# The class row joins the recurrent layer's output in TensorE's accumulation, instead of being added on GpSimd

## The reference

```python
ewma = (forward_ewma(x) + backward_ewma(x)) * 0.5
h = ewma @ W.T + b                               # 256 features
hidden = layernorm(h)
for l in range(2):                               # recurrent layers of 64 states
    delta = softplus(hidden @ Wd[l] + bd[l]); u = hidden @ Wi[l] + bi[l]
    decay = exp(-delta * softplus(A_log[l])); drive = delta * u
    hs, final = scan(decay, drive)               # s = d * s + g over 750 positions
    y = hs @ Wo[l] + bo[l]
    class_state = final @ Ws[l] + bs[l]          # one row of 256 per sequence
    hidden = y + class_state[:, None, :]
h = h + hidden
x2 = layernorm(h)
out = h + shared_mlp(x2) + routed_mlp(x2)        # 16 experts, 4 of them per position
```

## Time and profile before

| what | us |
|---|---|
| three timed runs | 1349.87, 1364.24, 1368.43 |
| median | 1364.24 |
| profiled execution, its own time | 1353.63 |
| its span, first to last instruction | 1351.8 |
| TensorE busy | 1192.3 (88%) |
| VectorE busy | 943.9 (70%) |
| ScalarE busy | 549.4 (41%) |
| GpSimd busy | 479.7 (35%) |

### The profile page before, as it was taken

The page is one execution under the profiler, slowest core; times in us unless marked ns, Lnnn a source line. Parts: engine busy times, 40 slices in busy tenths (PEclk is TensorE's granted clock), DMA queues, the critical chain, the costliest instruction groups (busy, mean ns, idle before and its releaser), DMA issues.

```text
span 1351.8 us, 24750 instructions
## 1 busy us (share of the span) xinstructions
PE 1192.3 (88%) x7477; PEld 1075.1 (80%) x7477; DVE 943.9 (70%) x2326; ACT 549.4 (41%) x899; POOL 479.7 (35%) x329
## 2 busy tenths in 40 slices
PE   4469859978999799977999899977999899999997
PEld 3358648768987689866988789867988789899997
DVE  6886996986479865897578864797658763654443
ACT  1525623622455235432366235452355343223332
POOL 2053382153315432164403623173412712163333
PEclk8659878988999899998999899997899899999999
DMA  3230021022323112231222303231122312244331
GB/s 105 47 86 23 28 83 31 27 74 56 51 41 88 44 22 47 40 93 48 25 63 57 88 10 52 40 93 41 13 48 39 90 37 24 42 125 71 51 52 21
DMA packets 88288, 71.48 MB, mean 53 GB/s; under 512 B 39671, under 2 KB 82848, under 8 KB 88168
## 3 DMA queue, kind: packets, MB, share of 16 engines
q1 hardware_dynamic: 58832, 43.30, 11.9%
q0 software_dynamic: 26832, 26.06, 11.7%
q10 hardware_dynamic: 2504, 0.55, 0.2%
HBM read 31.36 MB, written 39.34 MB: 52 GB/s over the span
## 4 chain that ended last, share of the span: by engine, by line
PE 62%; DVE 14%; issue 10%; POOL 9%; ACT 4%; DMA 0%; POOLq 0%; ACTq 0%; DVEq 0%
PE gu_ps L1669 18%; PE gu_ps L1642 13%; PE d_ps L1729 9%; PE d_ps L1710 7%; POOL lists L767 4%; PE ch_ps L1619 3%; PE ch_ps L1697 3%; PE ch_ps L1550 2%; POOL h L764 2%; PE ch_ps L1689 1%; PE ch_ps L1568 1%; DVE states L1157 1%; PE ch_ps L1610 1%; POOL out_dram L786 1%; PE ch_ps L1580 1%
## 5 line engine op out<-in xcount | busy, mean ns | idle before, releaser
L786 POOL DMA_INDIRECT out_dram<-block_rows,entry x99 | 160.3, 1619 | 323.4 <-ACT block_rows L926 271.7
L1669 PE MATMUL gu_ps<-gu_hi,bx_hi 128*128 x792 | 247.0, 312 | 15.3 <-issue 15.2
L914 ACT ACTIVATE hid<-gu_ps 128x512 f32<-128x512 f32 (+1 forms) x195 | 115.0, 592 | 301.3 <-PE gu_ps L1669 207.5
L1669 PE MATMUL gu_ps<-gu_lo,bx_hi 128*128 x792 | 232.1, 293 | 0.0
L1669 PE MATMUL gu_ps<-gu_hi,bx_lo 128*128 x792 | 231.7, 293 | 0.0
L767 POOL DMA_INDIRECT lists<-records,pos x96 | 139.5, 1453 | 196.1 <-DVE pos L1338 170.6
L1710 PE MATMUL d_ps<-down,hid 128*125 128x256 f32 x768 | 188.8, 391 | 0.0
L1669 PEld LDWEIGHTS gu_ps<-gu_hi,bx_hi 128*128 128x128 f32 x792 | 158.3, 200 | 24.7 <-issue 23.3
L1710 PEld LDWEIGHTS d_ps<-down,hid 128*125 128x125 f32 x768 | 144.5, 196 | 20.3 <-issue 0.3
L1669 PEld LDWEIGHTS gu_ps<-gu_hi,bx_lo 128*128 128x128 f32 x792 | 159.2, 201 | 1.2
L1669 PEld LDWEIGHTS gu_ps<-gu_lo,bx_hi 128*128 128x128 f32 x792 | 158.1, 200 | 0.0
(11 more groups left out here) (279 smaller groups left out, 2922.1 us busy)
## 6 DMA issues: line engine op xcount, KB each, us to landing
block_rows<-lists SPq DMA_DIRECT2D x99, 128.0 KB, 4.7
out_dram<-h SPq DMA_DIRECT2D x24, 500.0 KB
t<-rstd_scratch SPq DMA_DIRECT2D x21, 250.0 KB, 4.8
x_in<-in_x_dram SPq DMA_DIRECT2D x8, 375.0 KB, 7.8
zt<-in_x_dram SPq DMA_DIRECT2D x7, 375.0 KB, 3.9
entry<-lists SPq DMA_DIRECT2D x99, 8.0 KB, 3.0
out_dram<-block_rows,entry POOLq DMA_INDIRECT x99, 3.9
lists<-records,pos POOLq DMA_INDIRECT x96, 4.4
```

Source lines behind the costliest of these rows:

```text
L786: pool.indirect_dma_start(out=out_rows[0:there, :], out_offset=bass.IndirectOffsetOnAxis(entry[n % UE][:, ID:ID + 1].bitcast(U32), 0), in_ ...
L914: inc(act.activation(hid[g % 4][:, 0:n], gu_ps[:, 2 * (g % 2), 0:n], ACT.Silu), "silu_done")
L1669: last = pe.matmul(gu_ps[:, 2 * (g % 2) + half, q * GH:(q + 1) * GH], a[n % 2][:, k, :], w[:, k, bass.ds(of, 1), half * GH:(half + 1) * GH ...
```

## The change

`residual` is gone. TensorE makes the class row on one partition only. DVE adds the bias on one partition, rounds it (`rows` row 0) and stores what the rounding left (`rows` row 32); rows 1 to 31 of `rows` are zero. `row_one` is a constant with ones in rows 0 and 32. In every `y` product, once per group of 125 positions, one more matmul of `row_one` and `rows` (33 partitions, 256 columns) adds the row in the bank. So `y` on TensorE now waits for `row_ev`, and the copies of the next pair's norm rows to `t` wait for it too, since `row_sum` lies in `t`. The three tables are written anew.

```diff
-    ("ewma_back", 0, dict(DVE=-32.0)),
+    ("ewma_back", 0, dict(DVE=-30.0)),
-    ("residual", 0, dict(POOL=-6.5)),
-    ("residual", 1, dict(POOL=-6.5)),
...
-    ("y", (0, 0), dict(PE=-5.5, DVE=-5.5)),
-    ("y", (0, 1), dict(PE=-5.0, DVE=-4.5)),
-    ("ln2_stats", 0, dict(DVE=-4.5, POOL=-4.0)),
+    ("y", (0, 0), dict(PE=-6.0, DVE=-5.5)),
+    ("y", (0, 1), dict(PE=-5.5, DVE=-4.5)),
+    ("ln2_stats", 0, dict(DVE=-4.5, POOL=-7.0)),
...
-        brow = sb("brow", [TP, D])
-        rows = sb("rows", [TP, 2, D])
+        ROW_K = 33
+        brow = sb("brow", [1, D])
+        rows = sb("rows", [ROW_K, 2, D], F32R)
+        row_sum = t2[0:1, 0:2 * D].rearrange("p (b d) -> p b d", b=2)
+        row_one = sb("row_one", [ROW_K, TP], F32R)
...
-                    wait(sp, "row_mm", pair)
+                    wait(sp, "row_ev", pair)
...
-                elif step == "residual":
-                    wait(pool, "row_ev", pair + 1)
-                    hv = h_of[pair % 2][:, 2 * arg:2 * arg + 2, :]
-                    row = rows[:, arg // 3, :].unsqueeze(1).broadcast_to([TP, 2, D])
-                    inc(pool.tensor_tensor(hv, hv, row, ALU.add), "res_done")
...
-                    wait(dve, "res_done", 6 * pair)
-                    inc(dve.tensor_tensor(rows[:], ch(step, arg, pair)[0:TP, :].rearrange("p (b d) -> p b d", b=2),
-                                          brow[:, :].unsqueeze(1).broadcast_to([TP, 2, D]), ALU.add), "row_ev")
+                    wait(dve, "y_mm", 6 * pair)
+                    inc(dve.tensor_tensor(row_sum, ch(step, arg, pair)[0:1, :].rearrange("p (b d) -> p b d", b=2),
+                                          brow[:, :].unsqueeze(1).broadcast_to([1, 2, D]), ALU.add), "row_sum")
+                    wait(dve, "row_sum", pair + 1)
+                    inc(dve.tensor_copy(rows[0:1, :, :], row_sum), "row_hi")
+                    wait(dve, "row_hi", pair + 1)
+                    inc(dve.tensor_tensor(rows[ROW_K - 1:ROW_K, :, :], row_sum, rows[0:1, :, :].bitcast(F32),
+                                          ALU.subtract), "row_ev")
...
-                        last = pe.matmul(bank[0:TP, b * D:(b + 1) * D],
-                                         t1[own, T - 1:T].broadcast_to([N, TP]), ws1[own, :],
+                        last = pe.matmul(bank[0:1, b * D:(b + 1) * D], t1[own, T - 1:T], ws1[own, :],
                                          start=True, stop=True)
...
+                    wait(pe, "row_ev", pair + 1)
+                    wait(pe, "row_const", 4)
                     for n in range(2):
                         b, c0 = cols(t * SUB + 2 * q + n)
                         for w in (wo_hi, wo_lo):
-                            last = pe.matmul(bank[0:TP, n * D:(n + 1) * D], states[:, b, c0:c0 + TP], w[:],
-                                             start=(w is wo_hi), stop=(w is wo_lo))
+                            pe.matmul(bank[0:TP, n * D:(n + 1) * D], states[:, b, c0:c0 + TP], w[:],
+                                      start=(w is wo_hi), stop=False)
+                        last = pe.matmul(bank[0:TP, n * D:(n + 1) * D], row_one[:], rows[:, b, :], start=False,
+                                         stop=True)
```

More of the change, by code:

```diff
@@ L28 @@
     ("tok", 2, dict(PE=-26.5, DVE=-26.5)),
-    ("tok", 3, dict(PE=-25.0, DVE=-25.0)),
+    ("ewma_back", 1, dict(DVE=-28.5)),
+    ("tok", 3, dict(PE=-26.0, DVE=-26.0)),
     ("pre", (0, 0), dict(PE=-19.5, DVE=-19.5)),
-    ("pre", (0, 1), dict(PE=-18.5, DVE=-18.5)),
     ("split", (0, 0), dict(ACT=-13.0, DVE=-14.0)),
-    ("carry", 0, dict(PE=-12.5, DVE=-13.0)),
+    ("split", (0, 1), dict(ACT=-13.0, DVE=-13.0)),
+    ("carry", 0, dict(PE=-13.0, DVE=-13.5)),
+    ("ln1_stats", 0, dict(DVE=-23.0, POOL=-24.0)),
@@ L34 @@
+    ("rstd_row", 0, dict(PE=-23.5, ACT=-23.0)),
+    ("pre", (0, 1), dict(PE=-19.0, DVE=-18.5)),
+    ("rstd_row", 2, dict(PE=-23.0, ACT=-22.5)),
     ("tok", 4, dict(PE=-25.0, DVE=-25.0)),
-    ("split", (0, 1), dict(ACT=-13.0, DVE=-13.0)),
-    ("ln1_stats", 0, dict(DVE=-23.0, POOL=-24.5)),
+    ("spread", 0, dict(SP=-16.5)),
+    ("tok", 5, dict(PE=-24.0, DVE=-24.0)),
     ("pre", (0, 2), dict(PE=-18.5, DVE=-18.5)),
+    ("rstd_t", 0, dict(PE=-21.0, ACT=-21.5)),
     ("ssm_log", 0, dict(ACT=-18.0, DVE=-17.5)),
-    ("rstd_row", 0, dict(PE=-22.0, ACT=-21.5)),
@@ L68 @@
[L68 to L72 removed]
+    ("y", (1, 1), dict(PE=-4.5, DVE=-4.5)),
+    ("ln2_norm", 0, dict(DVE=-4.5, ACT=-4.0)),
+    ("ln2_norm", 1, dict(DVE=-2.0, ACT=-2.0)),
+    ("y", (2, 0), dict(PE=-2.0, DVE=-2.0)),
+    ("ln2_stats", 1, dict(DVE=-3.0, POOL=-2.0)),
+    ("ln2_stats", 2, dict(DVE=0.0, POOL=-2.0)),
@@ L116 @@
+    ("list", 6, dict(POOL=16.5)),
+    ("list", 8, dict(POOL=16.5)),
+    ("list", 9, dict(POOL=21.0)),
+    ("table", 0, dict(DVE=15.0)),
+    ("list", 10, dict(POOL=21.0)),
     ("table", 1, dict(DVE=15.5)),
     ("table", 2, dict(DVE=16.0)),
+    ("table", 3, dict(DVE=17.0)),
     ("route_weights", 0, dict(DVE=13.0)),
-    ("table", 3, dict(DVE=17.0)),
-    ("list", 11, dict(POOL=19.5)),
+    ("list", 11, dict(POOL=21.0)),
 )
@@ L168 @@
     (0, "x2t", (0, 0)): dict(ACT=-3.5),
-    (2, "list", 11): dict(POOL=20.5),
+    (2, "list", 11): dict(POOL=18.5),
+    (1, "list", 9): dict(POOL=16.5),
+    (1, "ewma_back", 0): dict(DVE=-32.5),
+    (1, "pre", (1, 1)): dict(PE=-11.0, DVE=-11.0, ACT=-10.5),
+    (1, "ssm_scan", 0): dict(DVE=-15.0),
+    (1, "pre", (1, 0)): dict(DVE=-13.0),
+    (1, "score_exp", 0): dict(ACT=4.5),
+    (0, "spread", 0): dict(SP=-23.5),
+    (1, "list", 0): dict(POOL=11.5),
+    (1, "spread", 0): dict(SP=-26.0),
+    (0, "split", (1, 0)): dict(ACT=-6.5, DVE=-8.0),
+    (1, "rstd_row", 1): dict(PE=-23.5),
+    (0, "carry", 0): dict(DVE=-14.0),
+    (0, "ewma", 1): dict(SP=-24.0),
+    (0, "pre", (1, 0)): dict(DVE=-13.0),
+    (0, "pre", (1, 1)): dict(DVE=-12.5),
+    (0, "ssm_decay", 1): dict(DVE=-10.0),
+    (0, "pre", (1, 2)): dict(DVE=-12.0),
+    (0, "ssm_scan", 1): dict(DVE=-9.5),
+    (0, "ssm_log", 1): dict(DVE=-11.0),
+    (0, "class_row", 0): dict(DVE=-8.0),
+    (0, "split", (1, 1)): dict(DVE=-7.5),
+    (1, "ln2_stats", 0): dict(POOL=-3.0),
+    (1, "ln2_stats", 1): dict(POOL=-1.0),
+    (1, "ln2_stats", 2): dict(POOL=-0.5),
+    (1, "ewma", 0): dict(POOL=-28.0, DVE=-39.5),
+    (1, "ewma", 1): dict(POOL=-26.0),
+    (0, "x2t", (1, 0)): dict(PE=0.5, ACT=0.5, DVE=0.5),
+    (0, "x2t", (1, 1)): dict(PE=1.0, ACT=1.0, DVE=1.0),
+    (0, "score_exp", 0): dict(ACT=5.5),
+    (0, "list", 1): dict(POOL=12.5),
+    (0, "list", 2): dict(POOL=13.5),
+    (0, "route_marks", 2): dict(DVE=12.0),
+    (0, "place_sum", 0): dict(DVE=11.0),
+    (0, "route_pick", 0): dict(DVE=9.0),
+    (1, "list", 7): dict(POOL=14.0),
 }
@@ L542, in bank_is_free @@
             elif was == "class_row":
-                wait(pe, "row_ev", pair + 1)
+                wait(pe, "row_sum", pair + 1)
             elif was == "y":
@@ L974, in _ @@
             inc(dve.memset(mhalf[:], -0.5), "const_done")
+            inc(dve.memset(rows[:, :, :].bitcast(F32), 0.0), "row_const")
+            inc(dve.memset(row_one[:].bitcast(F32), 0.0), "row_const")
+            dve.wait_ge(S["row_const"], 2)
+            for k in (0, ROW_K - 1):
+                inc(dve.memset(row_one[k:k + 1, :].bitcast(F32), 1.0), "row_const")
             dve.wait_ge(S["const_done"], 2)
@@ L1003, in prepare @@
                     inc(dve.tensor_tensor(bsum[:], bcol[:, :, 0], bcol[:, :, 1], ALU.add), "fold_ev")
-                    inc(dve.tensor_tensor(brow[:], brow[:], rows[:, 0, :], ALU.add), "fold_ev")
+                    inc(dve.tensor_tensor(brow[:], brow[:], bs_row, ALU.add), "fold_ev")
                     inc(dve.tensor_copy(wo_hi[:], wo_raw), "wo_hi_done")
@@ L1170, in chain @@
                     wait(dve, "y_mm", 6 * pair + 2 * t + q + 1)
-                    wait(dve, "res_done", 6 * pair + 2 * t + q + 1)
                     hv = h_of[pair % 2][:, j:j + 2, :]
```

137 lines of the change are left out of this document (58 added, 79 removed).

## The result

| | us |
|---|---|
| before, median of 20 runs | 1361.76 (1349.57 to 1368.71) |
| after, median of 20 runs | 1353.65 (1349.19 to 1359.44) |
| ratio after / before | 0.9945, 95% interval 0.9921 to 0.9968 |
| profiled execution of after, its own time | 1355.64 |
| forecast | 1339 (1314 to 1362) |

The change gains 8 us, 0.6%, where 19 to 23 were forecast. The profiled execution of before was 8 us quicker than its median, that of after 2 us slower, so the two profiles by themselves show no gain at all.

The account below looks back on a forecast made before the run. VectorE, held by GpSimd's residual bursts, was taken to set the stretches' length. Gains 14.3 + 3 + 6 - 4 = 19.3 us gave 1334 from the profiled 1353.6, 1345 carried to the median; between them 1339 us, range 1314 to 1362.

Parts of the forecast that it names:

- the added product: TensorE's `y` step: 96 more matmuls, at most a full one's price each, cost 4 us (0 to 20).
- The cover: Eight of a pair's twelve added products lie in the stretch, under TensorE's 8 idle us, hidden by VectorE's lag.
- Residuals removed, pairs 3 to 6: 14.3: Class row to low parts: four stretches fall from 175.1 to 160.8 us, gaining 14.3 (0 to 23).
- the class row's three instructions: VectorE's class row: one instruction becomes three, adding 1.3 us per pair (0.3 to 1.6).
- the scan of 1.8: VectorE's backward scan, moved behind the second split into the stretch: 1.78 us more for each of pairs 3 to 6.
- more than that: Rival, chance 0.31: each vanished wait also saves a half-clock stretch; 34 us gained, 1320 us.
- Pair 7: 3: Pair 7: removing the stall of VectorE's table instruction gains 3 us (0 to 6).
- Pairs 0 to 2: 6: Pairs 0 to 2: shorter splits and `nmr`, earlier average addition, less 1.3 per pair; gain 6 us (-4 to 12).
- Nothing gained: Rival, chance 0.14: other GpSimd work holds VectorE (14 us), TensorE pays all 96 products (11.5); 1356 us.
- the sign of being wrong: Forecast fails if a VectorE instruction beside GpSimd's power and addition grows to 3 us; one of three such signs.
- The page's length of the stall: Rival, chance 0.05: a split waits for only one residual, 1.3 us, and pair 3's long stretch stays; 1358 us.
- Slower: the SiLU behind the average: Rival, chance 0.07: ScalarE's SiLU behind the `ew_hi` copy starts 5 us later, TensorE loses 42 us; 1376 us.

Follow-up runs that it names:

- 64 and 65 rows: Changed kernel with the added product's operands 64 or 65 partitions deep instead of 33; one run each: 1353.77 us with 64, 1324.02 with 65.
- with 128 rows: Changed kernel with the added product's two operands 128 partitions deep instead of 33, extra rows zero; 1323.13 us, ratio 0.9757.
- the kernel with the old start: Changed kernel, products 128 deep, with pairs 0 and 1 and weight preparation at the places of before, less residuals; 1319.01 us, ratio 0.9717.

## Why the prediction was wrong

**The step that failed: the added product, "-4 (0 to -20)".** It costs 30 to 36 us. The sum put "no row shows that depth, so the price stands between 0 and that of a full one" under it, as if a shallower product could only be cheaper, and added that "the weight load of each hides behind the matmul before, as now". It doesn't: the load of 33 rows begins only with its own product, and so does the load of 128 rows behind it. And the trace of before has a shallow product, the class row's own, 64 rows deep, and I did not look at it. PE of before, pair 5:

```profile
744.27 0.38 PE L1710 MATMUL d_ps<-down,hid 128*125 128x256 f32 x1
744.58 1.44 PE L1596 MATMUL ch_ps<-ws,t 64*125 64x256 f32 x4
745.95 0.38 PE L1669 MATMUL gu_ps<-gu_hi,bx_hi 128*128 x1
746.17 0.28 PE L1669 MATMUL gu_ps<-gu_hi,bx_lo 128*128 x1
```

0.31 us into it, 1.37 for four of them (0.34 each), and 0.22 for the matmul behind, where 0.12 is the rule: the price of the change of depth stood there. By these three distances one such product between two of 128 rows would cost 0.31 + 0.34 + 0.22 less the 0.24 of its neighbours without it, an estimate of 0.63 us, or 60 us for 96 if all are exposed. By the distances of the changed kernel it is 0.38 + 0.12 = 0.50 and 48 us, of which 30 to 36 came.

The Trainium skill has the rule that I left out. "TensorEngine Tiling (Array Packing)", sections "Tiling Modes" and "Key Properties", lists modes of 32, 64 and 128 rows and says that changing the mode drains TensorE. The runs agree that 64 and 65 rows lie on two sides, and a product across that line costs 0.38 us more here. The Trainium skill's "TensorE: Matmul & The Clock Gate", section "Step-by-step: what each phase is for", says that the row count doesn't matter for the time of a weight load. The listed loads agree (180 ns at 33 rows, 180 to 190 at 128); when a load begins does depend on it, 0.32 us after the one before for 0.12.

**The cover.** Eight of twelve products were to hide under VectorE's lag. For the depth's part that held for the most in the stretches: with 128 rows they are 151.8 us, with 33 156.3, 1.1 a pair for 8 x 0.38 = 3.0. The other four products a pair stand where TensorE is dense and paid in full: pairs 3 to 6 lose 12.4 us, 3.1 a pair, of which 2.0 lie outside the stretch, where four times 0.38 = 1.5 were to be had. For the product as such, at 0.12 us, the term of 4 was about right: 5.2 to 7.0.

**Residuals removed, pairs 3 to 6: 14.3.** The stretches gained 16.8 by the profile (156.3 for 173.1), with the forecast's parts near: the class row's three instructions end 1.85 us after the first begins, 1.2 more than before (1.3); `nmr` is back at 0.14; the scan of 1.8 lies inside. The step was too low by more than half: without the product pairs 3 to 6 gain 32.2 us (594.0 for 626.2), 22.5 of them in the stretches and the rest behind them; the removal alone, in the old order, gains 20.7. The span without the product is 34.2 us shorter, near the rival "more than that", which had 36 if its 2 us for the product are left out. Each stall is also followed by a stretch at half clock, and before's profiled execution had one stall less than the second one. That rival had the mechanism right and fell, in the main, by the price of the product. Its 6 us for pairs 0 to 2 did not come either.

**Pair 7: 3.** The stretch from its class row to the low parts is 29.8 us for 33.7, right. From there to the end, though, the profile of after is 2.9 us longer (295.0 for 292.1): it has a standstill of ScalarE that this profile of before has not, told below.

**Pairs 0 to 2: 6.** A gain is there in the kernel with the old start, 5.3 us (428.2 for 433.5; 2.5 against the second profile of before). The removal alone is worth more, 15.0 (418.5); the rest of the change takes it back. The changed kernel instead is 14.9 later than before: 10.2 by the depth (448.4 for 438.2, though its second profile shows 4.9) and 10.0 by the new places (438.2 for 428.2), which I had costed at nothing. Putting back ScalarE's two copies alone brings 6.1 of these 10.0 (432.1). Another of the places is in VectorE's rows: the first backward scan stands at 9.83 us behind a weight product's addition that waits 2.43, where before it began at 7.67.

**The other rivals.** "Nothing gained" has nearly the right time, 1356, by a wrong way: it let TensorE pay 11.5 us and other bursts 14. VectorE's new waits of that kind are 1.6 us in pairs 4 to 6, beside GpSimd's low part, and 1.4 and 0.8 in pair 3. The scan there takes 3.38 us, though beside the low part and not, as the sign of being wrong had it, beside the power and the addition. "The page's length of the stall": a single GpSimd instruction holds VectorE to its end, 1.6 to 2.0 us, near what the Trainium skill's "SBUF — State Buffer", section "Who interferes with whom", has, but a burst without a gap holds it throughout. Its 1358 is excluded by what the bursts cost, at least 13 us. "Slower: the SiLU behind the average": in pair 5 ScalarE's copy waited 6.30 us for GpSimd and the SiLU began at 769.74, 19.3 us after the class row, where it began 13.1 after it before and I had worked out 18.1; and pairs 3 to 6 don't lose by it (597.1 and 597.7). What the copies' places cost ahead of pair 3 is told above.

**Luck.** The time lies inside the stated range only because two errors of opposite sign met: removal and new order together were worth about twice the 14.3 us in pairs 3 to 6, and the product cost 30 to 36 us for 4.

## What to carry to other kernels

Before adding a small matmul to a dense stream, look for any shallow product in the trace and read the distances on both sides of it; if they are long, pad the operands with zero rows to the depth of the neighbours. Where a VectorE instruction with its inputs in SBUF stands near a run of GpSimd instructions, move the step that releases them behind it: here that one move gave 37 us, nearly all that the additions cost, where rewriting the sum gave 8. And take a second profile of a kernel whose runs scatter: a wait that hangs on some tenths of a us can be there in one and not in the other.
